# A conditioned block and a mixture of experts in one kernel: the prologue's network, its loads and batch 1's norm rearranged

## What is computed

```python
h = silu(noise_encoding(t, 128) @ W1 + b1) @ W2 + b2      # the conditioning network, all batches
scale, shift = h @ Wsc + bsc, h @ Wsh + bsh
# block A: the norm is over all 512 x 512 numbers of a batch
out = silu(scale * layer_norm(x, gamma, beta) + shift) @ W_in + b_in
out = silu(scale * layer_norm(out, gamma, beta) + shift) @ W_out + b_out
x = out + x
# block B: the expert of the batch, hidden size 2048
h = gelu(x @ Wi[e] + bi[e])
r = h @ Wo[e] + bo[e] + x
y = (r - mean(r)) * rsqrt(var(r) + 1e-12) * gamma[e] + beta[e]   # mean and var by row
```

## Time and profile before

| | us |
|---|---|
| median of 3 runs | 1807.51 (1807.16 to 1808.1) |
| the profiled execution | 1807.46 |
| its span, first to last instruction | 1805.3 |
| TensorE busy in the span | 1771.7 (98%) |
| VectorE, ScalarE, POOL busy | 1291.2, 979.3, 110.5 |
| mean granted TensorE clock | 0.992 |

### The profile page before, as it was taken

The page is one execution under the profiler, slowest core; times in us unless marked ns, Lnnn a source line. Parts: engine busy times, 40 slices in busy tenths (PEclk is TensorE's granted clock), DMA queues, the critical chain, the costliest instruction groups (busy, mean ns, idle before and its releaser), DMA issues.

```text
span 1805.3 us, 21906 instructions
## 1 busy us (share of the span) xinstructions
PE 1771.7 (98%) x7757; PEld 1457.0 (81%) x7757; DVE 1291.2 (72%) x2143; ACT 979.3 (54%) x1550; POOL 110.5 (6%) x200
## 2 busy tenths in 40 slices
PE   7799999999999999999999999999999999999997
PEld 4688888888888888888888888888888888888886
DVE  6666777767777777777767777777776777767565
ACT  4545556554565645556554565545555554555442
POOL 1000000100000000000000000000000000000001
PEclk9899999999999999999999999999999999999999
DMA  7132143233323333143233323323133232322321
GB/s 286 27 120 85 54 144 101 97 108 120 106 73 121 108 101 122 53 141 110 97 108 103 123 73 120 108 97 110 69 122 124 103 109 82 142 76 90 112 93 58
DMA packets 46909, 189.31 MB, mean 105 GB/s; under 512 B 7314, under 2 KB 7314, under 8 KB 30418
## 3 DMA queue, kind: packets, MB, share of 16 engines
q1 hardware_dynamic: 44402, 183.96, 28.9%
q0 software_dynamic: 2400, 3.97, 1.7%
HBM read 171.10 MB, written 16.81 MB: 104 GB/s over the span
## 4 chain that ended last, share of the span: by engine, by line
PE 96%; DVE 2%; issue 1%; ACT 1%; DMA 0%; DVEq 0%; SPq 0%; POOL 0%; ACTq 0%
PE out_acc L407 39%; PE hid_ps L407 38%; PE blk_ps L407 18%; PE hid_ps L364 0%; DVE bn L652 0%; PE blk_ps L364 0%; DMA x<-in_xT 0%; ACT work L556 0%; DVE work L697 0%; DVE bn_r L771 0%; DVE h_lo L640 0%; DVE r_sb L766 0%; DVE mlp_turned L819 0%; DVE work L707 0%; DVE x L720 0%
## 5 line engine op out<-in xcount | busy, mean ns | idle before, releaser
L407 PE MATMUL hid_ps<-x_hi,wi_hi 128*128 128x512 f32 x1024 | 398.6, 389 | 0.1
L407 PE MATMUL hid_ps<-x_lo,wi_hi 128*128 128x512 f32 x1024 | 398.4, 389 | 0.0
L407 PE MATMUL hid_ps<-x_hi,wi_lo 128*128 128x512 f32 x1024 | 398.4, 389 | 0.0
L407 PE MATMUL out_acc<-wo_hi,g_hi 128*128 128x512 f32 x1024 | 398.3, 389 | 0.0
L407 PE MATMUL out_acc<-wo_lo,g_hi 128*128 128x512 f32 x1024 | 398.3, 389 | 0.0
L407 PE MATMUL out_acc<-wo_hi,g_lo 128*128 128x512 f32 x1024 | 398.3, 389 | 0.0
L546 ACT ACTIVATE g_sb<-hid_ps,bi_sb 128x512 f32<-128x512 f32 x256 | 175.9, 687 | 325.8 <-PE hid_ps L407 325.4
L640 DVE TENSOR_TENSOR g_lo<-g_sb,g_hi 128x512 fp32r<-128x512 f32 x256 | 175.2, 684 | 197.7 <-ACT g_hi L550 196.0
L506 ACT ACTIVATE wo_hi<-stage 128x512 fp32r<-128x512 f32 x256 | 161.9, 632 | 178.7 <-PE out_acc L407 178.7
L640 DVE TENSOR_TENSOR wo_lo<-stage,wo_hi 128x512 fp32r<-128x512 f32 x256 | 176.5, 689 | 72.7 <-ACT wo_hi L506 69.3
L407 PEld LDWEIGHTS hid_ps<-x_hi,wi_hi 128*128 128x128 f32 x1024 | 192.3, 188 | 40.6 <-DVE x_lo L640 0.8
(11 more groups left out here) (94 smaller groups left out, 1668.6 us busy)
## 6 DMA issues: line engine op xcount, KB each, us to landing
stage<-in_expert_w SPq DMA_DIRECT2D x128, 1024.0 KB, 4.9
x<-in_xT SPq DMA_DIRECT2D x16, 1024.0 KB, 6.5
out_y<-r_sb SPq DMA_DIRECT2D x15, 1024.0 KB, 5.3
rows<-in_expert_rows SPq DMA_DIRECT2D x16, 512.0 KB, 6.9
mv_all<-mv_dram POOLq DMA_DIRECT2D x30, 128.0 KB, 4.1
stage<-in_W SPq DMA_DIRECT2D x1, 1024.0 KB, 7.2
gamma_sb<-in_gammaT SPq DMA_DIRECT2D x4, 256.0 KB, 10.1
beta_sb<-in_betaT SPq DMA_DIRECT2D x4, 256.0 KB, 9.8
```

Of the source, the lines that this page charges most:

```text
L407: last = pe.matmul(dst, w[wp], xs[xp], start=start and i == 0, stop=stop and i == 2)
```

## The change

- **Network.** `group` replaces `layer`: a 128 x 128 piece of the weight matrix is the stationary side, the vectors are the moving side, padded with zeros to 112 columns (`WIDE`). The result has features on partitions. The transposes are gone; ScalarE adds the bias on its way out of PSUM (`cond_part`), feature chunk by feature chunk. Wsc and Wsh are packed by output chunk (`cond_w`), and chunk 3 of scale and shift is computed within the first block.
- **Loads.** W2 ahead of x, x in four chunks, gamma and beta packed into one load a chunk, then network and layer chunks in the order of need. The token index comes behind W_out, with a semaphore of its own.
- **First layer of batch 0.** VectorE goes chunk by chunk through `centre`, `affine`, W_in's remainder and `h_lo`; POOL's part is gone. TensorE takes the block chunk by chunk.
- **Second norm of batch 0.** Statistics directly after the evacuations, other order of `centre` and `affine`, more warming products.
- **Batch 1.** Its first norm leaves the prologue: the table `STAGE_AT_1` puts totals and `centre` into tick 1, `affine` into 2, SiLU into 3, `h_hi` and `h_lo` into 4, the four tiles of W_in into ticks 5, 5, 6, 6, the totals of the second norm into 8. Its statistics stand behind batch 0's `h_lo`. Other batches keep their ticks.
- **ScalarE.** `silu` has a second wait. `bo_part` of batch 0 goes to tick 1, the table load for GELU ahead of `x2_hi`.

```diff
@@ block_a_due
+STAGE_AT_1 = STAGE_AT | {X_STATS: (), X_TOTALS: (1,), X_CENTRE: (1,), X_AFFINE: (2,),
+                         X_SILU: (3,), X_SPLIT: (4,), W_IN: (5, 5, 6, 6), A_TOTALS: (8,)}
@@ tensor
-            def layer(bank, src, w):
+            def group(bank, n, w, src):
                 for c in range(DC):
-                    last = pe.matmul(bank[0:BLOCK, :], src[:, c, :], w[:, c, :],
+                    last = pe.matmul(bank[:, n * WIDE:(n + 1) * WIDE], w[:, c, :], src[:, c, :],
                                      start=(c == 0), stop=(c == DC - 1))
                 return last
...
-            first_block(0, 0)
-            keep_warm(blk_ps[1], 4)
+            first_block(0, 0, [(m, 0) for m in range(DC)])
+            scale_of(DC - 1)
+            shift_of(DC - 1)
+            first_block(0, 0, [(m, c) for c in range(1, DC) for m in range(DC)])
+            keep_warm(blk_ps[1], 8)
@@ scalar
             def silu(b, which, c):
                 at = work[:, c, :]
+                act.wait_ge(s_cond, 2 * (c + 1) if turn_of(b, which) == 0 else 2 * DC)
                 act.wait_ge(s_aff, DC * turn_of(b, which) + c + 1)
                 act.activation(at, at, ACT.Silu, scale=scale_sb[:, c, b:b + 1],
                                bias=shift_sb[:, c, b:b + 1]).then_inc(s_silu, 1)
...
-            for c in range(2):
-                w_hi_part(0, c)
-            act.wait_ge(s_cond, 2)
             for c in range(DC):
+                w_hi_part(0, c)
+                scale_shift(c)
                 norm_end(0, 0, [c])
-                if c + 2 < DC:
-                    w_hi_part(0, c + 2)
@@ vector
+            for c in range(DC):
+                centre(0, 0, c)
+                affine(0, 0, c)
+                w_lo_part(0, c)
+                h_lo_part(0, 0, c)
+            w_lo_part(1, 0)
+            w_lo_part(1, 1)
+            for m in range(DC):
+                stats(0, 1, m)
...
-            totals(1, 0)
-            for c in range(DC):
-                centre(1, 0, c)
```

More of the change, by code:

```diff
@@ L73, with block_a_due @@
 BLOCK = 32
+WIDE = 112
 QUADS = [(h, s) for h in range(P // BLOCK) for s in range(P // BLOCK)]
-STATS_TURN = [0, 2, 1] + list(range(3, 2 * B))
-def stats_turn(b, which):
-    return STATS_TURN[2 * b + which]
 def turn_of(b, which):
     return 2 * b + which
[L89 to L95, removed]
+def block_a_due(k, stage):
+    for b in range(1, B):
+        for m, at in enumerate((STAGE_AT_1 if b == 1 else STAGE_AT)[stage]):
+            if k == HT * (b - 1) + at:
+                yield b, m
 def last_norm_due(k, at):
@@ L112, in const_columns, with build @@
     return np.stack([np.concatenate([freq, freq]), turns, radians], axis=1).astype(np.float32)
-def build(nc, xT, t, itok, consts, small, W1, W2, Wsc, Wsh, gammaT, betaT, W_in, W_out,
+def build(nc, xT, t, itok, consts, small, W1, W2, cond_w, affine, W_in, W_out,
           expert_w, expert_bi, expert_rows, mv_dram, y):
@@ L388, in _ @@
             last.then_inc(s_mm1, 1)
+            keep_warm(hid_ps[0], 5)
+            pe.wait_ge(s_pad, 1)
+            pe.wait_ge(ld_w2, 16)
+            pe.wait_ge(s_m1, DC)
+            for m in range(DC):
+                last = group(blk_ps[1 - m // 2], m % 2, w2_raw[:, :, m * P:(m + 1) * P], m1)
+                if m % 2:
+                    last.then_inc(s_mm2, 1)
             pe.wait_ge(s_average, 1)
@@ L415, in block_products, with first_block @@
                              (h_hi[:, c, :], h_lo[:, c, :]), start=(c == 0), stop=(c == DC - 1))
-            def first_block(b, which):
-                order = [(m, c) for c in range(DC // 2) for m in range(DC)] + \
-                        [(m, c) for m in range(DC) for c in range(DC // 2, DC)]
+            def first_block(b, which, order):
                 for m, c in order:
@@ L602, in _ @@
                 a_evac(0, m)
+            for c in range(DC // 2, DC):
+                w_hi_part(1, c)
             for k in range(FIRST_PAIR):
@@ L811, in _ @@
             dve.tensor_scalar(red, tmp, -PI_BELOW, None, ALU.max).then_inc(s_enc, 1)
[L813 to L832, removed]
             def w_lo_part(n, c):
@@ L865, in _ @@
             wi_lo_part(1)
+            wo_lo_part(0)
             wo_lo_part(1)
-            totals(1, 0)
-            for c in range(DC):
-                centre(1, 0, c)
             for k in ticks:
@@ L1017 @@
                                 axis=1),
-        "W1": A["W1"], "W2": A["W2"], "Wsc": A["Wsc"], "Wsh": A["Wsh"],
-        "gammaT": A["gamma"].T, "betaT": A["beta"].T,
+        "W1": A["W1"], "W2": A["W2"],
+        "cond_w": np.stack([A["Wsc"], A["Wsh"]]).reshape(2, DC, P, DC, P).transpose(3, 2, 0, 1, 4)
+                    .reshape(DC, P, 2 * DC * P),
+        "affine": np.stack([A["gamma"].T, A["beta"].T]).reshape(2, DC, P, S).transpose(1, 2, 0, 3)
+                    .reshape(DC, P, 2 * S),
         "W_in": A["W_in"], "W_out": A["W_out"],
```

218 lines of the change are left out of this document (124 added, 94 removed).

## The result

The change takes 1816.57 us (median of 5 runs, 1816.4 to 1818.49) against 1807.92 us before (1807.16 to 1808.56): ratio 1.005, interval 1.0036 to 1.0065. It is slower, as forecast, by 8.7 us where 4.4 were forecast; 1816.57 lies inside the range, but above the 1809 to 1815 that the prediction gave the forecast by itself. The profiled execution took 1816.67 us around a span of 1814.8.

What follows compares the result with a forecast made beforehand. TensorE is busy throughout from 83.0 to 1790 us, so all gain lies ahead of 83 us. Steps 1 to 3 save 22.1, step 4 loses 26.5: 1807.5 - 22.1 + 26.5 = 1811.9 us; range 1803 to 1819.

Steps and rivals of the forecast that it cites:

- Step 1: Network and first norm of batch 0: last evacuation of the first block at 33.2 instead of 42.34, gain 9.1 us.
- the clock's rival: Prologue: TensorE's clock falls to 0.50 during W2 alone, costing 1.5 us; part of a rival with chance 0.13 together.
- Step 2: Second norm of batch 0: earlier statistics 1.0, warming products 0.4; `h_lo` releases TensorE at 41.3 instead of 51.69, 10.4 in all.
- Step 3: Batch 1 out of the prologue: third up-projection begins at once after the second, 11.65 us gone.
- Step 4: silu's second wait holds 29 SiLU table loads in the ticks; TensorE idles 0.92 us each, 26.5 us lost.
- The load was not free: Rival: ScalarE's queue runs the table load ahead of the separate wait, so no loss in the ticks: 1785.4; chance 0.15.
- Nor did anything idle behind it: Rival: something idle behind each table load stretches its delay as far as 2.73 us: 1852 us; chance 0.02.
- Narrow passes or clock: Rival, prologue: passes at 0.21 give 1819.7; clock at 0.50 during W2 costs 1.5; or late expert pair; together 0.13.
- Batch 1's totals: Rival: VectorE's tick 1 wait for these takes batch 1's place, 5 of 22 us stay lost: 1817; chance 0.08.
- the rival of the slow passes: Network at 0.21 us a pass: first 40 cost 3.6 more, TensorE bounds first block for another 4.2: 1819.7; within 0.13.

Runs made afterwards that it cites:

- swapped kernel: The change with silu's two waits exchanged, s_aff written first and s_cond second, against the change; 1786.47 us, ratio to before 0.9886.
- tile order: The change with silu's two waits exchanged, plus the first block's products of chunks 2 and 3 tile by tile instead of chunk by chunk; 1790.26 us.

## Why the prediction was right, and by how much it was off

- **What bounds it** held: nothing was gained in the ticks, all of it before 83 us.
- **Step 1** (9.1) was 1.3 too high: the last evacuation began at 34.5, not 33.2. The passes (0.119 for 0.12), the chain of a chunk (`h_lo` every 3.82 us) and the end by the chain were right; the landing of W2 was not. The prediction took x's landing at 7.53 for it and named the 12 KB of biases ahead of W2, but put W2's landing at 7.8, 0.3 us for them. By bytes they are nothing, but they are 128 rows of 96 bytes. Moved behind, they let the network start when the SiLU allows, and the clock's rival lost its occasion. That these rows make the dip is shown; how they do it isn't.
- **Step 2**: `h_lo` released TensorE at 42.9 instead of 41.3, which is step 1's 1.3 and 0.3 of its own. The 0.4 us given to the warming products could not be seen. In the swapped kernel's execution the release came at 42.35, so that there steps 1 and 2 gave 9.3 of the 10.4.
- **Step 3** (11.65): by the traces the time between the second block's first product and the third projection fell from 31.31 to 16.97 us, which less one tile of 2.72 is 11.6. On its own the step measured 11.3, and only with three shifts of the change, of which the prediction had said no more than that "ScalarE's and VectorE's parts of the third projection come some 1 us early". Without them 2.3 us of the gain would have stayed away (9.0): the sum of this step held, but hung on a condition that it did not price.
- Together the steps gave 21.1 us (1807.6 to 1786.5) of 22.1. The 1.0 that is missing is that of steps 1 and 2.
- **Step 4** named the mechanism and its count, 29. The load's price, the slack and the stall (0.92, measured 0.90) held. The term that was missing is what TensorE loses after a stall: 0.13 us a group, 3.8 in all. With it 29 x 1.03 = 29.9, measured 30.1 between the two orders of the waits and 29.6 in the ticks alone. (The prediction's product is a little off too: 29 x 0.92 is 26.7, not 26.5.)
- **Rivals.** The load was not free. Nor did anything idle behind it: held, it delayed the SiLU by 1.35 us with its 1.283. The Trainium skill's 2.66 a switch (ScalarE: Activation LUTs, "What ACT_TABLE_LOAD costs") is seen in no run; batch 1's wait rose by 1.3 in the kernel before with the wait added. *Narrow passes or clock* did not happen in the change, but it was near: with 32 columns, or W2 later still, it does. Batch 1's totals held nobody.

The change took 4.7 us more than the sum: 3.6 of step 4 and 1.0 of the prologue. (As a difference to before the miss is 4.3, since the median of before was 1807.5 in one set of runs and 1807.9 in the other.) Both misses went the same way, and step 4's loss was 0.11 us a group off where the prediction allowed 0.03. The range held because it had been stretched to 1819 for the rival of the slow passes, which did not happen.

## What to carry to other kernels

Where an engine's function table changes, look at the order of the waits ahead of the first instruction that needs it: one may go with the instruction, the other stands ahead of the load. Let the one that is long fulfilled be the one ahead of the load, or touch the table before waiting. Read this from the order of the instructions and not from the source: here the wait written last stood ahead. Price a stall of TensorE with its restart. Do not take a small load ahead of a large one as free because it has few bytes; whether the rows, the bytes or the place in the queue make its price was not separated here. A wait that covers other lateness must not be removed without asking what is late next.

## What was not expected of the hardware

- The same two waits in either order differ by 30.1 us in 1800.
- 12 KB in rows of 96 bytes ahead of a load of 1 MB: 112 to 263 GB/s for 1.5 us in seven profiled executions, against 338 to 399 in the three with the rows elsewhere, and W2 was waited for from 0.9 to 2.0 us.
- An idle TensorE behaved in two ways: 2.65 us without any product left the clock at 1.00 (fewer warming products), while after 2.39 us (tile order) it was 0.50 soon after the restart. These are one execution each, and what tells the two apart stays open.
- Padding moving columns with zeros from 32 to 112 left a pass at 0.119 us (0.112 with 16 columns) and kept the granted clock at 1.00: 6.5 us.
